# Bias addition on VectorE and x1's stores on ScalarE, instead of both on GpSimd, in a two-layer graph kernel

## Chip, cores and metric

The kernel runs on one core of a Trainium2 chip. The metric is the device time of one execution in microseconds (us), lower being better. The engines are called by the names in the profile: PE is TensorE, PEld its weight loads, DVE is VectorE, ACT is ScalarE, POOL is GpSimd and SP is SyncE, which here only issues DMAs.

## What is computed

```
h  = relu(layernorm(x))                       # x is 1250 x 1024, float32
W  = zeros(1024, 1024).at[src, dst].add(edge_weight)
x  = x + (h @ W.T + bias)                     # "x1" below
h  = relu(layernorm(x))
# two neighbour-averaging layers; A[d, s] = number of edges s -> d, deg = row sums of A
h1 = relu(h @ W_self0 + (A @ h / max(deg, 1)) @ W_neigh0 + b0)
o  = h1 @ W_self1 + (A @ h1 / max(deg, 1)) @ W_neigh1 + b1
return x + o
```

There are 40000 edges, sorted by destination. All matrices are float32.

## The kernel before

The program has four stages on one timeline. **Build** (0 to about 100 us): one-hot rows and PE matmuls turn the edge list into the columns of W and of A. The partial sums of A, 288 small windows in 45 units, are written to a DRAM scratch (`asum_scratch`). **Turn** (about 100 to 119 us): W is transposed. **Mixing** (to about 232 us): for each of 10 tiles of 128 nodes (`TN` = 10), h0 = relu(x - mean) is transposed and multiplied with W, x1 is formed, normalised into `hn`, transposed and written to `hT_scratch`. **Dense steps and layers** (to the end): each layer does its weight products in 7 x 5 steps v (`PAIRS` = 5), then the products with A.

The order on each engine is written out by hand. In the mixing it follows `mix_order()`: for tile i the steps A(i+2) (moments of x, and h0), M(i) (PE's 48 matmuls), T1(i-1) (transposes of hn), T0(i+2) (transposes of h0), B(i) (x1 and its normalisation). Each engine has its own part of each step:

- DVE in B(i), L1634 to L1645: waits for M(i) (`s_mm`) and for the biased x (`s_xb`), and from tile 2 for the store that last read this x1 buffer (`s_x1d`). It then computes x1 = bank * rstd + x in two halves (L1638), the moments of x1 (L1478 to L1483), and after ACT's square root (L899) the reciprocal (L1487) and `less` (L1645). The following A step takes the moments of a later x tile.
- ACT in B(i): issues the load of x tile i+4, takes the root, and computes hn (L927). In A it computes h0 (L921), named h in the trace. In T1(i-1) it copies the transposed hn out of PSUM (L998), stores it (L1001), and splits a weight block for the first dense steps (L1013; DVE does the other half, L1622).
- POOL adds the bias to each x tile (L792), issues the store of x1 two tiles back (`store_x1b`, L565), and makes A's additions (L783): each adds one window of the summed partials, loaded to `az` in units of 4 to 12 windows, to the table AT at an offset that it reads from a small table. `add_asums(slot)` makes the additions of one slot; slot 0 is before the mixing, slots 1 to 10 are the tiles and slots 11 to 15 the first five dense steps. `TURN_ADDS` and `MIX_ADDS` set how many additions each slot holds.
- SP issues loads in one queue. The unit loads of `az` (L670) of a slot come at that slot's place among the weight block loads (L605), and each waits until POOL has used up the unit four before it (the ring `az` has NZ = 4 buffers). The first two operand loads of the dense steps (L623, `stage<-hT_scratch`) stand in this queue behind the unit loads of slot 10.

Dense step 0 needs its operand split into two halves: ACT makes the high half (L1022), POOL the low half (L827, `operand_lo(0)`), which in POOL's order stands behind the additions of slot 10. In ACT's order `operand_hi(0)` stands in T1(8), behind hn of tile 8, and `operand_hi(1)` behind hn of tile 9. Product v is 24 matmuls (L1317). PE waits for both halves, for x1 of the tile whose PSUM banks it takes, and for the eight weight blocks.

Of the kernel before, what the change touches and what calls it, by code (L numbers as in the profile page):

```python
# [55 lines left out]
NCONST = 12 + len(set(WDS))  # L56
SETS = [(0, 8), (8, 11), (11, 13), (13, 15), (15, 17)] + [(j, j + 1) for j in range(17, NG)]
SET_OF = {j: w for w, (a, b) in enumerate(SETS) for j in range(a, b)}
TURN_ADDS = 36
MIX_ADDS = 21  # L60
FIRST_DEG = 27
EPS = 1e-5
EXACT = 4096
# [39 lines left out]
def build_program(nc, x, dst, src_cols, dst_cols, weight_cols, L0_gnn_bias, L1_gnn_W_self0, L1_gnn_W_neigh0,  # L103
# [10 lines left out]
    with ctx:  # L114
# [167 lines left out]
        s_lom = sem("s_lom")  # L282
        s_lo = sem("s_lo")
        s_mm = sem("s_mm")
        s_xb = sem("s_xb")
        s_less = sem("s_less")
        s_norm = sem("s_norm")
        s_bb = sem("s_bb")
# [271 lines left out]
            n = rows_of(i)  # L560
            eng.dma_start(x_tile(i)[0:n, :], x[NT * i:NT * i + n, :]).then_inc(s_x[i % NX], 16)

        def store_x1b(pool, i):
            pool.wait_ge(s_x1, i + 1)
            pool.dma_start(x1b_d[i], x1[:, i % 2, :]).then_inc(s_x1d[i % 2], 16)  # L565

        def store_out(pool, o):
            half, i = divmod(o - OL, TN)
# [149 lines left out]
        def _(pool):  # L718
# [66 lines left out]

            pool.wait_ge(s_tabd, 32)
            pool.wait_ge(s_built, 1)
            add_asums(0)
            pool.wait_ge(s_vec, 16)
            for i in range(TN):  # L790
                pool.wait_ge(s_h0, i + 1)
                pool.tensor_tensor(x_tile(i), x_tile(i), bias[:, :], ALU.add).then_inc(s_xb, 1)  # L792
                if i >= 2:
                    store_x1b(pool, i - 2)
                add_asums(i + 1)


            def add_operands(v):
# [64 lines left out]
            operand_lo(0)  # L863
            for layer in range(2):
                for v in range(VL * layer, VL * (layer + 1)):
                    if v < 2:
                        store_x1b(pool, TN - 2 + v)
                    if v + 1 < VL * (layer + 1) and v != VL:
                        add_operands(v + 1)
                        operand_lo(v + 1)  # L870
                    add_asums(1 + TN + v)
                    for c in blocks_at(v):
                        add_blocks(c)
                    for k in g_at(layer, v % VL - 1):
                        g_lo(k)
                for k in g_at(layer, VL - 1):
                    g_lo(k)
                for o in range(OL):
                    if layer == 1 and o == 0:
                        base_and_b1(0)  # L880
                    if layer == 1 and o >= 1:
                        store_out(pool, OL + o - 1)
                    if layer == 1 and o + 1 < OL:
                        base_and_b1(o + 1)
                    for k in g_between(layer, o):
                        g_lo(k)
                    if layer == 0 and o == OL - 1:
                        operand_lo(VL)
                        operand_lo(VL + 1)
# [5 lines left out]
        def _(act):  # L895
# [128 lines left out]
            for what, i in mix_order()[EARLY_STEPS:]:  # L1024
                if what == "A":
                    above_mean(i)
                    root_of(0, i)
                elif what == "B":
                    if i + NX < TN:
                        act.wait_ge(s_x1, i + 1)  # L1030
                        load_x(act, i + NX)
                    root_of(1, i)
                    normalize_x1(i)
                elif what == "T0":
                    h0_hi(i)
                elif what == "T1":
                    if i == TN - 2:
                        operand_hi(0)
                    hT_out(i)
                    if i < WB:  # L1040
                        block_hi(i)
# [348 lines left out]
        def _(dve):  # L1390
# [8 lines left out]
            def link(ins):  # L1399
                dve.wait_ge(s_dve, tick(ins))  # L1400
# [223 lines left out]
            for what, i in mix_order()[EARLY_STEPS:]:  # L1624
                if what == "A":
                    mix_A(i)
                elif what == "T0":
                    h0_lo(i)
                    inverse_std(0, i)
                elif what == "B":  # L1630
                    dve.wait_ge(s_mm, i + 1)
                    dve.wait_ge(s_xb, i + 1)
                    if i >= 2:
                        dve.wait_ge(s_x1d[i % 2], used(i - 2, 2))  # L1634
                        dve.wait_ge(s_hn, i - 1)
                    for half in range(2):
                        part = slice(HF * half, HF * (half + 1))
                        last = dve.scalar_tensor_tensor(out=x1[:, i % 2, part], in0=bank[2 * (i % 2) + half][0:NT, :],  # L1638
                                                        scalar=rstd[:, 0, i:i + 1], in1=x_tile(i)[:, part],
                                                        op0=ALU.mult, op1=ALU.add)  # L1640
                    last.then_inc(s_x1, 1)
                    dve.wait_ge(s_x1, i + 1)
                    moments(x1[:, i % 2, :], 1, i)
                    inverse_std(1, i)
                    dve.scalar_tensor_tensor(out=less[:, 1, i:i + 1], in0=mv[:, 1, i, 0:1], scalar=-1.0,  # L1645
                                             in1=rstd[:, 1, i:i + 1], op0=ALU.mult, op1=ALU.mult).then_inc(s_norm, 1)
                elif what == "T1":
                    if i < WB:
                        block_lo(i)
# [150 lines left out]
```

## Time and profile before

| what | value |
|---|---|
| median of 3 runs | 843.28 us (840.98 to 848.15) |
| profiled execution, its own time | 841.92 us |
| its span in the profile | 840.2 us |
| granted PE clock, mean | 0.991 of full |
| busy: PE, PEld, DVE, ACT, POOL | 799.4, 649.0, 456.5, 377.5, 431.8 us |

The span leaves out 1.7 us of the profiled execution's time. PE is busy for 95% of the span, and the other engines for 45 to 54%, so time can be saved where PE is idle or where its clock is below full.

### The profile page before, as it was taken

What the parts mean: (1) busy time and instruction counts of PE and PEld (TensorE: products, weight loads), DVE (VectorE), ACT (ScalarE), POOL (GpSimd) and SP (SyncE); (2) the same over time, 40 slices, a digit from 0 to 9 for tenths busy, and PEclk for the clock granted to TensorE, in tenths of its full rate; (3) what the DMA queues carried; (4) which work ended last, traced back from release to release, by engine and by line L of the source; (5) the groups of instructions that cost most, each with busy time, mean ns of one, the idle gap of its engine ahead of it and who ended that gap; (6) DMA issues with size and microseconds to landing.
All of it is one profiled execution on the core that took longest, in us unless ns stands there. A gap on an engine that the chain in (4) does not pass through costs nothing.

```text
span 840.2 us, 13554 instructions
## 1 busy us (share of the span) xinstructions
PE 799.4 (95%) x4660; PEld 649.0 (77%) x4661; DVE 456.5 (54%) x769; ACT 377.5 (45%) x491; POOL 431.8 (51%) x599
## 2 busy tenths in 40 slices
PE   3999999999969999999999999999999999989996
PEld 2667788888858877888877888888878887868785
DVE  7999665655532456757922453234558656224333
ACT  6755644344234322233236876453222323256652
POOL 3000047677767688765751210115888657655642
PEclk9999999999989999999999999999999999999998
DMA  3122333554376773567855543547833768666653
GB/s 107 45 68 83 92 121 115 202 174 133 123 258 190 248 251 130 168 207 252 279 185 189 191 161 114 182 136 239 293 126 113 239 220 305 217 213 189 230 179 107
DMA packets 82489, 148.58 MB, mean 177 GB/s; under 512 B 9983, under 2 KB 21366, under 8 KB 82416
## 3 DMA queue, kind: packets, MB, share of 16 engines
q1 hardware_dynamic: 62394, 102.47, 38.4%
q10 hardware_dynamic: 16982, 34.81, 11.4%
q0 software_dynamic: 3040, 10.36, 3.2%
q8 instruction: 41, 0.67, 0.3%
q14 instruction: 32, 0.26, 0.1%
HBM read 100.34 MB, written 47.27 MB: 176 GB/s over the span
## 4 chain that ended last, share of the span: by engine, by line
PE 60%; POOL 15%; issue 9%; DVE 6%; DMA 3%; ACT 3%; POOLq 1%; ACTq 1%; SPq 0%; DVEq 0%
PE bank L1317 32%; PE bank L1345 17%; POOL AT L783 6%; PE bank L1172 3%; PE bank L1161 3%; POOL T L842 2%; ACT split L1022 1%; POOL S L809 1%; PE bank L1156 1%; POOL T L844 1%; PE bank L1361 1%; DMA az<-asum_scratch 1%; DVE L L1517 1%; PE bank L1254 1%; POOLq L783 1%
## 5 line engine op out<-in xcount | busy, mean ns | idle before, releaser
L1317 PE MATMUL bank<-slot,split 128*128 128x512 f32 x1680 | 387.6, 392 | 11.3 <-ACT split L1022 10.6
L1317 PEld LDWEIGHTS bank<-slot,split 128*128 128x128 f32 x1680 | 315.5, 189 | 79.8 <-issue 14.5
L783 POOL TENSOR_TENSOR AT<-AT,az 128x50 int32 (+3 forms) x288 | 80.2, 279 | 133.3 <-DMA az<-asum_scratch 93.6
L827 POOL TENSOR_TENSOR split<-stage,split 128x512 fp32r<-128x512 f32 x50 | 64.6, 1293 | 130.7 <-ACT split L1022 130.7
L1622 DVE TENSOR_TENSOR slot<-T,slot 128x512 fp32r<-128x512 f32 x64 | 69.7, 1089 | 95.2 <-ACT slot L1013 91.8
L1052 ACT CAST Ax<-AT 128x1280 fp32r<-128x1280 uint16 x40 | 106.5, 2662 | 29.8 <-PE bank L1345 18.7
L1622 DVE TENSOR_TENSOR slot<-wst,slot 128x512 fp32r<-128x512 f32 x48 | 49.6, 1054 | 100.1 <-ACT slot L1013 100.1
L1013 ACT CAST slot<-T 128x512 fp32r<-128x512 f32 x64 | 39.8, 622 | 123.9 <-POOL T L844 92.9
L1254 PE MATMUL bank<-slot,split_m 128*128 128x512 f32 x320 | 89.4, 394 | 0.0
L1728 DVE SCALAR_TENSOR_TENSOR cst<-bank,dinv,stage 128x512 f32<-128x512 f32 x40 | 29.9, 749 | 102.8 <-PE bank L1345 69.1
L1345 PE MATMUL bank<-slot,Ax 128*128 128x512 f32 x320 | 77.1, 393 | 0.0
L1345 PEld LDWEIGHTS bank<-slot,Ax 128*128 128x128 f32 x320 | 59.3, 188 | 12.2
L1254 PEld LDWEIGHTS bank<-slot,split_m 128*128 128x128 f32 x320 | 59.0, 188 | 11.4
L844 POOL TENSOR_TENSOR T<-T,wst 128x512 f32<-128x512 f32 x48 | 61.3, 1293 | 0.0
L1022 ACT CAST split<-stage 128x512 fp32r<-128x512 f32 x50 | 31.1, 623 | 65.7 <-POOL stage L818 25.8
L1156 PE MATMUL bank<-L,R 125*128 125x100 bf16 (+3 forms) x320 | 45.7, 197 | 8.3 <-DVE L L1517 8.0
L1345 PE MATMUL bank<-g_first,Ax 128*128 128x512 f32 x200 | 49.3, 393 | 0.0
L1254 PE MATMUL bank<-WTlo,split_m 128*128 128x512 f32 x160 | 49.3, 389 | 0.0
L1161 PE MATMUL bank<-L,R 125*128 125x80 bf16 (+3 forms) x960 | 47.3, 192 | 0.1
L1156 PEld LDWEIGHTS bank<-L,R 125*128 125x128 bf16 x320 | 31.5, 98 | 20.1 <-issue 14.0
L860 POOL TENSOR_TENSOR base<-base,b 128x512 f32<-128x512 f32 x20 | 25.8, 1294 | 40.1 <-DMA base<-x1b_scratch 32.2
L1161 PEld LDWEIGHTS bank<-L,R 125*128 125x128 bf16 x960 | 43.1, 99 | 4.0 <-issue 0.2
(172 smaller groups left out, 1084.6 us busy)
## 6 DMA issues: line engine op xcount, KB each, us to landing
stage<-hT_scratch SPq DMA_DIRECT2D x90, 256.0 KB, 3.2
wst<-in_L_gnn_W_neigh SPq DMA_DIRECT2D x56, 256.0 KB, 4.3
wst<-in_L_gnn_W_self SPq DMA_DIRECT2D x56, 256.0 KB, 3.5
hT_scratch<-hTs ACTq DMA_DIRECT2D x10, 512.0 KB, 3.1
x1b_scratch<-x POOLq DMA_DIRECT2D x10, 512.0 KB, 4.1
stage<-prod0s_scratch SPq DMA_DIRECT2D x20, 256.0 KB, 2.7
hT_scratch<-h1s ACTq DMA_DIRECT2D x20, 256.0 KB, 2.1
stage<-prod1s_scratch SPq DMA_DIRECT2D x20, 256.0 KB, 2.7
```

The lines of the kernel that those rows point to most:

```text
L783: pool.tensor_tensor(a, a, az32[:, n % NZ, pairs * pos:pairs * (pos + 1)], ALU.add) \
L827: pool.tensor_tensor(split[:, v % 2, 1, :], source(v), split[:, v % 2, 0, :].bitcast(F32), ALU.subtract).then_inc(s_olo, 1)
L844: last = pool.tensor_tensor(T[:, b, :], T[:, b, :], wst[:, c % NS, :], ALU.subtract)
L1013: act.copy(slot[t % 2][:, 0, HF * b:HF * (b + 1)], block_source(c)).then_inc(s_whi, 1)
L1022: act.copy(split[:, v % 2, 0, :], source(v)).then_inc(s_ohi, 1)
L1052: act.copy(Ax[:, o % 2, :, :], ATd[:, NT * n:NT * (n + 1), :].rearrange("p d s -> p s d")).then_inc(s_ax, 1)
L1156: last = pe.matmul(a_bank(n)[:, at:at + ka(j)], row, L[:, q, c, 0:ka(j)], start=(c % SHARED[j] == 0), stop=ends)
L1161: last = pe.matmul(w_bank(j)[:, bass.ds(offsets[c // SHARED[j]], kw(j))], row, L[:, q, c, ka(j) + kw(j) * part:ka(j) + kw(j) * (part + 1)] ...
L1254: last = pe.matmul(bank[2 * (i % 2) + half][0:NT, :], split_m[:, i % 2, a, NT * k:NT * (k + 1)], WT[b][:, k, HF * half:HF * (half + 1)], s ...
L1317: last = pe.matmul(dense_bank(v, which)[:, :], split[:, v % 2, a, NT * k:NT * (k + 1)], slot[t % 2][:, b, HF * (HK * which + k):HF * (HK * ...
L1345: last = pe.matmul(ag_bank(rest_o)[:, :], Ax[:, o % 2, s, :], g_parts(half, s)[:, b, :], start=(s == 0 and b == 0), stop=(s == TN - 1 and ...
L1622: dve.tensor_tensor(lo, block_source(c), hi.bitcast(F32), ALU.subtract).then_inc(s_wlo, 1)
```

## The change

VectorE adds the bias to x in step B, ahead of its waits for the product, with a wait of its own for the result. ScalarE issues the store of x1 of the same tile, in step B, behind a wait for x1. GpSimd has neither any more: from slot 0 to 10 it makes only additions. The slots are redistributed: 40 additions in slot 0 instead of 36, 23 in each tile's slot instead of 21, and so 18 in the five dense slots together instead of 42. The same 288 additions are made. SP's unit loads move with their slots.

```diff
--- before.py
+++ after.py
@@ -56,8 +56,8 @@
 NCONST = 12 + len(set(WDS))
 SETS = [(0, 8), (8, 11), (11, 13), (13, 15), (15, 17)] + [(j, j + 1) for j in range(17, NG)]
 SET_OF = {j: w for w, (a, b) in enumerate(SETS) for j in range(a, b)}
-TURN_ADDS = 36
-MIX_ADDS = 21
+TURN_ADDS = 40
+MIX_ADDS = 23
 FIRST_DEG = 27
 EPS = 1e-5
 EXACT = 4096
@@ -282,7 +282,6 @@
         s_lom = sem("s_lom")
         s_lo = sem("s_lo")
         s_mm = sem("s_mm")
-        s_xb = sem("s_xb")
         s_less = sem("s_less")
         s_norm = sem("s_norm")
         s_bb = sem("s_bb")
@@ -560,9 +559,8 @@
             n = rows_of(i)
             eng.dma_start(x_tile(i)[0:n, :], x[NT * i:NT * i + n, :]).then_inc(s_x[i % NX], 16)
 
-        def store_x1b(pool, i):
-            pool.wait_ge(s_x1, i + 1)
-            pool.dma_start(x1b_d[i], x1[:, i % 2, :]).then_inc(s_x1d[i % 2], 16)
+        def store_x1b(eng, i):
+            eng.dma_start(x1b_d[i], x1[:, i % 2, :]).then_inc(s_x1d[i % 2], 16)
 
         def store_out(pool, o):
             half, i = divmod(o - OL, TN)
@@ -785,14 +783,8 @@
 
             pool.wait_ge(s_tabd, 32)
             pool.wait_ge(s_built, 1)
-            add_asums(0)
-            pool.wait_ge(s_vec, 16)
-            for i in range(TN):
-                pool.wait_ge(s_h0, i + 1)
-                pool.tensor_tensor(x_tile(i), x_tile(i), bias[:, :], ALU.add).then_inc(s_xb, 1)
-                if i >= 2:
-                    store_x1b(pool, i - 2)
-                add_asums(i + 1)
+            for slot_of_adds in range(TN + 1):
+                add_asums(slot_of_adds)
 
 
             def add_operands(v):
@@ -863,8 +855,6 @@
             operand_lo(0)
             for layer in range(2):
                 for v in range(VL * layer, VL * (layer + 1)):
-                    if v < 2:
-                        store_x1b(pool, TN - 2 + v)
                     if v + 1 < VL * (layer + 1) and v != VL:
                         add_operands(v + 1)
                         operand_lo(v + 1)
@@ -1026,9 +1016,10 @@
                     above_mean(i)
                     root_of(0, i)
                 elif what == "B":
+                    act.wait_ge(s_x1, i + 1)
                     if i + NX < TN:
-                        act.wait_ge(s_x1, i + 1)
                         load_x(act, i + NX)
+                    store_x1b(act, i)
                     root_of(1, i)
                     normalize_x1(i)
                 elif what == "T0":
@@ -1628,8 +1619,11 @@
                     h0_lo(i)
                     inverse_std(0, i)
                 elif what == "B":
+                    if i == 0:
+                        dve.wait_ge(s_vec, 16)
+                    dve.wait_ge(s_h0, i + 1)
+                    link(dve.tensor_tensor(x_tile(i), x_tile(i), bias[:, :], ALU.add))
                     dve.wait_ge(s_mm, i + 1)
-                    dve.wait_ge(s_xb, i + 1)
                     if i >= 2:
                         dve.wait_ge(s_x1d[i % 2], used(i - 2, 2))
                         dve.wait_ge(s_hn, i - 1)
```

ACT's order in the last two tiles, from the weight block of tile 7's step to the split of dense step 1's operand. Before:

```order
233 L1013 CAST slot0<-wst 128x512
234 L899 ACTIVATE std<-var 128x1
235 L927 ACTIVATE hn<-x1,less,rstd 128x1024
236 L1022 CAST split<-stage 128x512
237 L998 COPY hTs<-bank6 128x512
238 L998 COPY hTs<-bank7 128x512
239 L1001 DMA hT0_scratch<-hTs 128x1024
240 L899 ACTIVATE std<-var 128x1
241 L927 ACTIVATE hn<-x1,less,rstd 128x1024
242 L1022 CAST split<-stage 128x512
```

After:

```order
241 L1003 CAST slot0<-wst 128x512
242 L563 DMA x1b_scratch<-x1 128x1024
243 L889 ACTIVATE std<-var 128x1
244 L917 ACTIVATE hn<-x1,less,rstd 128x1024
245 L1012 CAST split<-stage 128x512
246 L988 COPY hTs<-bank6 128x512
247 L988 COPY hTs<-bank7 128x512
248 L991 DMA hT0_scratch<-hTs 128x1024
249 L563 DMA x1b_scratch<-x1 128x1024
250 L889 ACTIVATE std<-var 128x1
251 L917 ACTIVATE hn<-x1,less,rstd 128x1024
252 L1012 CAST split<-stage 128x512
```

A store of x1 now stands ahead of each root, behind the store of the transposed hn. On POOL, nothing but additions stands ahead of the first operand's low half any more.

DVE's order for tile 8, from `less` of tile 7. Before:

```order
366 L1645 SCALAR_TENSOR_TENSOR less<-mv,rstd 128x1
367 L1622 TENSOR_TENSOR slot0<-wst,slot0 128x512
368 L1638 SCALAR_TENSOR_TENSOR x1<-bank0,rstd,xt 128x512
369 L1638 SCALAR_TENSOR_TENSOR x1<-bank1,rstd,xt 128x512
370 L1478 BN_STATS st<-x1 128x6 x2
371 L1480 BN_AGGR mv<-st 128x2
372 L1483 TENSOR_SCALAR var<-mv 128x1
373 L1487 RECIPROCAL rstd<-std 128x1
```

After:

```order
374 L1639 SCALAR_TENSOR_TENSOR less<-mv,rstd 128x1
375 L1613 TENSOR_TENSOR slot0<-wst,slot0 128x512
376 L1625 TENSOR_TENSOR xt<-xt,bias 128x1024
377 L1632 SCALAR_TENSOR_TENSOR x1<-bank0,rstd,xt 128x512
378 L1632 SCALAR_TENSOR_TENSOR x1<-bank1,rstd,xt 128x512
379 L1469 BN_STATS st<-x1 128x6 x2
380 L1471 BN_AGGR mv<-st 128x2
381 L1474 TENSOR_SCALAR var<-mv 128x1
382 L1478 RECIPROCAL rstd<-std 128x1
```

One instruction, the bias addition over 1024 columns, has come in behind the weight block's low half and ahead of x1.

SP's order around the first operand loads (`stage<-hT0_scratch`). Before:

```order
26 L605 DMA wst<-in_L1_gnn_W_self0 128x512
27 L670 DMA az<-asum_scratch 128x480 x6
28 L670 DMA az<-asum_scratch 128x160
29 L670 DMA az<-asum_scratch 128x500 x13
30 L623 DMA stage<-hT0_scratch 128x512 x2
31 L670 DMA az<-asum_scratch 128x500
32 L605 DMA wst<-in_L1_gnn_W_neigh0 128x512 x2
33 L623 DMA stage<-hT0_scratch 128x512
```

After:

```order
26 L603 DMA wst<-in_L1_gnn_W_self0 128x512
27 L668 DMA az<-asum_scratch 128x480 x4
28 L668 DMA az<-asum_scratch 128x160
29 L668 DMA az<-asum_scratch 128x500 x18
30 L621 DMA stage<-hT0_scratch 128x512 x2
31 L603 DMA wst<-in_L1_gnn_W_neigh0 128x512 x2
32 L621 DMA stage<-hT0_scratch 128x512
33 L668 DMA az<-asum_scratch 128x500
```

Ahead of the two operand loads now stand 18 loads of the widest units where there were 13.

## Rows read from the trace of the kernel before

**Rows 1.** Windows of the whole core; columns are named in the first line.

```profile
core 0: us, PE busy (x) PEld busy (x) DVE busy (x) ACT busy (x) POOL busy (x), PEclk, DMA share, GB/s
...
110.00:232.80 122.80, 122.80 (x624) 103.58 (x622) 69.03 (x152) 48.48 (x82) 85.97 (x236) 1.00 0.46 152
232.80:240.08 7.28, 0.01 (x1) 0.03 (x1) 3.49 (x9) 4.21 (x8) 5.38 (x16) 0.84 0.74 251
240.08:253.22 13.14, 13.14 (x48) 10.60 (x49) 5.00 (x4) 3.01 (x6) 7.96 (x15) 0.83 0.78 258
253.22:327.00 73.78, 72.06 (x321) 59.18 (x319) 32.96 (x38) 25.37 (x44) 57.08 (x68) 1.00 0.66 215
```

**Rows 2.** Waits of PE in the whole span: line, releaser, us, times, longest.

```profile
PE bank L1317 <- ACT split L1022: 10.6, 4, 7.3
```

**Rows 3.** Timeline of PE: start, us, line, operation, count, idle before and releaser.

```profile
181.97 1.03 PE L1177 MATMUL bank<-ident,hn 128*128 128x128 f32 x8
...
194.61 1.03 PE L1177 MATMUL bank<-ident,hn 128*128 128x128 f32 x8
...
231.77 1.03 PE L1177 MATMUL bank<-ident,hn 128*128 128x128 f32 x8
...
240.08 13.30 PE L1317 MATMUL bank<-slot,split 128*128 128x512 f32 x48 [7.28 <-ACT split L1022]
...
254.01 43.78 PE L1317 MATMUL bank<-slot,split 128*128 128x512 f32 x192
```

**Rows 4.** Timeline of PEld, the weight loads, around 195 us.

```profile
195.38 0.90 PEld L1177 LDWEIGHTS bank<-ident,h 128*128 128x128 f32 x8
```

**Rows 5.** Timeline of POOL at the end of the mixing.

```profile
227.35 2.40 POOL L792 TENSOR_TENSOR xt<-xt,bias 128x1024 f32<-128x1024 f32 x1
229.69 0.57 POOL L565 DMA_DIRECT2D x1b_scratch<-x  x1
...
238.60 1.28 POOL L827 TENSOR_TENSOR split<-stage,split 128x512 fp32r<-128x512 f32 x1
```

**Rows 6.** Timeline of SP, the DMA issues.

```profile
173.72 58.30 SPq L670 DMA_DIRECT2D az<-asum_scratch  x20
232.11 0.86 SPq L623 DMA_DIRECT2D stage<-hT_scratch  x2
```

**Rows 7.** Timeline of ACT.

```profile
191.37 1.25 ACT L927 ACTIVATE hn<-x,less,rstd 128x1024 f32<-128x1024 f32 x1 [0.42 <-DVE less L1645]
193.00 1.15 ACT L921 ACTIVATE h<-xt,less 128x1024 f32<-128x1024 f32 x1 [0.38 <-DVE less L1482]
...
229.79 1.24 ACT L927 ACTIVATE hn<-x,less,rstd 128x1024 f32<-128x1024 f32 x1 [2.56 <-DVE less L1645]
235.04 0.62 ACT L1022 CAST split<-stage 128x512 fp32r<-128x512 f32 x1 [4.01 <-DMA stage<-hT_scratch]
```

**Rows 8.** Timeline of DVE.

```profile
185.17 0.69 DVE L1622 TENSOR_TENSOR slot<-wst,slot 128x512 fp32r<-128x512 f32 x1 [4.72 <-ACT slot L1013]
...
187.55 1.41 DVE L1638 SCALAR_TENSOR_TENSOR x<-bank,rstd,xt 128x512 f32<-128x512 f32 x2
...
227.46 2.30 DVE L1645 SCALAR_TENSOR_TENSOR less<-mv,rstd 128x1 f32<-128x1 f32 x1
232.80 1.41 DVE L1638 SCALAR_TENSOR_TENSOR x<-bank,rstd,xt 128x512 f32<-128x512 f32 x2 [3.04 <-DMA x1b_scratch<-x]
```

**Rows 9.** One line's instructions: L783 from 126 to 238.59 us.

```profile
L783 POOL TENSOR_TENSOR AT<-AT,az x210: 216/256/751, 126.0 to 238.3; 128x30 int32 x32, 128x50 int32 x31, 128x40 int32 x28, 128x20 int32 x14
```

**Rows 10.** The tile bias, and the tensor x1b_scratch, by line.

```profile
L792 POOL TENSOR_TENSOR xt<-xt,bias x8: 2377/2400/2410, 121.3 to 227.3; 128x1024 f32<-128x1024 f32 x8
...
L565 POOL DMA_DIRECT2D x1b_scratch<-x x10: 571/573/747, 145.6 to 245.2; - x10
```

**Rows 11.** Timeline of POOL, two additions that DVE's 185.17 row overlaps.

```profile
184.91 1.08 POOL L783 TENSOR_TENSOR AT<-AT,az 128x40 int32 x2
```

**Rows 12.** DVE's groups by line, 260 to 600 us, shapes apart.

```profile
L1730 DVE TENSOR_TENSOR cst<-cst,b 128x512 f32<-128x512 f32 x20 | 13.9, 693 | 0.7
```

## The prediction

> **What bounds the kernel now.** I read the windows first, then what PE waits for, then PE's timeline around its longest wait, then the other engines there.
>
> The windows [rows 1] show PE without a pause from 110 to 232.80 us. From 232.80 to 240.08 it does nothing. Then it needs 13.14 us for 48 matmuls, at a mean granted clock of 0.83, so part of that time is at the lower level of 1.2 GHz. After that it is nearly gapless at 1.00. PE's table of waits puts 10.6 us in the whole span down to L1317 and ACT's split, of which 7.3 us is this one wait [rows 2]. So the mixing is bound by PE, 12.64 us a tile (194.61 less 181.97), and the dense steps are too: 192 matmuls take 43.78 us, 5.47 us for a product of 24 [rows 3]. What can be won lies in the 20.4 us between 232.80 and 253.22: at full clock, two products need 10.94 us. That leaves 9.5 us: 7.28 idle and 2.2 of clock.
>
> Who is late there? The profile names ACT's split, but ACT had made that one by 235.66 [rows 7]. POOL makes the other half at 238.60, ending 239.88, 0.20 us before PE starts [rows 3, 5]. POOL did not wait; it came to the split when the additions ahead were done. ACT's own split was late because its operand was: SP issued that load at 232.11, at the end of 58 us in which its unit loads were paced by POOL's additions [rows 6]. ACT waited 4.01 us for it, and all that it does for tile 9 stood behind that [rows 7]. DVE too started x1 of tile 9 only at 232.80, after waiting for the store of tile 7, which POOL issued at 229.69 behind a bias addition [rows 5, 8]. All three threads lead to GpSimd being late at the end of the mixing.
>
> **GpSimd after the change.** From 126.0 to 238.6 us it made 210 additions [rows 9]. In these 112.6 us lie 9 bias additions of 2.40 us (21.6) and 8 stores of 0.57 us (4.6) [rows 10]. The rest, 86.4 us, is 0.411 us an addition with all pauses. In the changed kernel four units of 12 windows are loaded before the mixing instead of three, so 48 additions can be made before the next unit lands at about 126. 270 less 48 leaves 222, or 91.2 us, which ends at 217. DVE's new additions hold GpSimd up: while a two-input DVE instruction of 0.69 us ran, two of its additions took 1.08 us [rows 8, 11], where two at the median of 0.256 [rows 9] take 0.51; so 0.57 us, and about 1.0 us for one nearly twice as long. Nine of these make 226. SP keeps unit loads behind weight block loads until 173.7 [rows 6], which may cost another 1 or 2: 227 to 228. The low half is wanted at about 231, so 3 to 4 us are spare. The operand load, now behind 18 of the widest units instead of 13, is issued once 254 additions are made, some 16 before the end, near 221; with 3 us of transfer it is there 6 us early. Moving 24 additions forward thus costs nothing here as long as those 3 us hold. The 18 left in the dense steps lighten GpSimd where PE is the bound: nothing won.
>
> **VectorE's addition.** No row has this instruction. The nearest has two SBUF inputs and half the columns and takes 0.693 us [rows 12]; doubled it is 1.39, less a fixed part paid once. I take D = 1.25 us. The bounds are 0.69 (half the columns) and 2.40, what GpSimd needs for the same work [rows 10]. It stands in DVE's order behind the weight block and ahead of x1, so all of step B and the following step A come D later, unless DVE was waiting anyway. In a quiet tile h0 of the next but two is ready at 194.15 [rows 7] and PE loads it at 195.38 [rows 4]: 1.23 us of slack. D uses it up, and with the handover PE slips 0.1 to 0.2 us. But the chain starts at the transposes of hn (181.97) and ends one tile later: a slip gives the next chain that much more room, so it recurs every second tile. For the seven tiles concerned I count 0.3 us. For larger D the loss over the mixing is about half of (D - 1.25) in each of 8 tiles, 4 x (D - 1.25).
>
> Something is given back. In tile 8 DVE's `less`, a one-column instruction with two SBUF inputs, took 2.30 us from 227.46 and ended at 229.76, just as GpSimd's bias addition begun at 227.35 ended at 229.75 [rows 5, 8]. That blocking goes, so hn of tile 8, which ended at 231.03 [rows 7], should come about 0.8 us earlier (2.1 won, D lost), in time for its transposes at 231.77.
>
> Here a rule bears on the change. The Trainium skill, page "SBUF — State Buffer", section "Practical consequences", says that a DVE instruction with two SBUF inputs and a GpSimd instruction that reads SBUF exclude each other for a whole instruction, whichever issues first. By that rule, the 2.30 us row agrees. It speaks against the new addition as well: DVE would first sit out the addition in progress, and GpSimd then stand still for all of D. The rows at 185.17 show DVE's 0.69 us, the same as the 0.693 us mean elsewhere, in the midst of GpSimd's additions [rows 8, 11, 12], so I charge DVE nothing for this in the sum, and a rival below takes the other case.
>
> **The stores.** SP issues two loads in 0.86 us [rows 6], so I take 0.4 us for a store on ACT. From x1's end (188.96) to hn's start (191.37) [rows 7, 8] ACT has only a load to issue and one root to take, so this costs nothing in a tile, and x1's buffer comes free two tiles early. In tile 9 the store follows the transposed hn's, still ahead of the root.
>
> **The end of the mixing, new.** PE ends the hn transposes at 232.80 as before (all times plus the 0.3 slip). ACT's high half of operand 0, behind hn of tile 8, is ready by 230.9, GpSimd's low half by 232.2. The rest that product 0 needs, x1 of tile 8 and eight weight blocks, comes ahead of hn of tile 8 in DVE's order. So it starts at 232.8, no longer at 240.08, and ends at 238.27. What is late next is product 1's operand, behind hn of tile 9. DVE can begin x1 at 232.0, right after the matmuls. From x1's start to hn's end a quiet tile takes 5.07 us (187.55 to 192.62) [rows 7, 8]: 237.1. ACT's split of 0.62 gives 237.7, GpSimd's 1.28 [rows 5] gives 239.0, the handover of 0.2 gives 239.2. PE pauses 0.9 us. Product 1 ends at 239.2 + 5.47 = 244.67, where before it was 253.22. I count on the clock staying up: it did after the pauses of 1.7 us in all between 253 and 327 [rows 1]. Of the 9.5 us, 8.55 are won; with the slip of 0.3 the gain is 8.25. Steps behind this wait on PE's progress, on rings and on each other in the same way as before, so all shifts as one.
>
> The profiled execution took 841.92 us, so 833.7 by its own time. The median shown is 1.36 us above it: 843.28 - 8.25 = **835.0 us**.
>
> **Rivals.**
> *GpSimd still late.* At 0.45 us an addition, or with more blocking, it reaches the low half near 235. Each microsecond beyond 231 costs one: gain 4.5, 838.8 us. For it: the 0.411 has pauses I can't place. Against: only at 238.6 would all be lost.
> *The port rule in full.* DVE sits out up to one addition of 0.26 us (the median in [rows 9]) before each bias addition: D = 1.5, 1 us more of slips: 836.0. The page is the one named above.
> *VectorE becomes the mixing's bound, and the kernel slower.* The place is h0 for PE's transposes. By the formula the gain is gone at D = 3.3 us. At D = 3.9, if a bias addition took as long as GpSimd's and half as much again in waits, the loss is 10.6 and the time 845.6. At D = 2.4 it is 4.6: 839.6. Against it: 0.693 us for half of it.
> *The wait does not go.* Another thread (weight blocks, transfers on ACT's queue, now with 512 KB more a tile) holds product 0 back by several us: 841 to 844. The DMA share, 0.74 in the idle window [rows 1], speaks a little for it, though five unit loads leave that neighbourhood.
> *More than counted.* No slips, product 1 in time: 833.8. If earlier stores and lighter dense steps also close the later pauses of 1.7 us: 832.1.
>
> **Chances.** The forecast, 834 to 836: 0.51. GpSimd late: 0.12. The port rule: 0.10. VectorE partly (to 843): 0.05; wholly (slower than before): 0.05. The wait stays: 0.07. More than counted: 0.10. A measurement of this kernel tells about 1% (8.4 us) from no change, and the forecast lies on that edge, at 0.98%. I give half of it to each side: faster by over 1% 0.26 + 0.10 + 0.02 = 0.38; slower by over 1% 0.04, from VectorE's case; the same 0.58. The range reaches down to 832 and up to 841, which leaves out the wait that stays and VectorE as the bound.
>
> **What would show it.** In the profile after: PE's wait near 233 us under 1 us and one of about 1 us near 238; no window at 0.83 clock behind it; GpSimd reaching its first split before 231; the first operand loads issued near 221; DVE's new line at 1.2 to 1.3 us; per-tile period of PE 12.65 to 12.75. A DVE mean above 2 us, a period above 13, or operand loads after 229 would make the prediction wrong.

## The result, and the profile after

| kernel | median | range of 5 runs | ratio to before, 95% interval |
|---|---|---|---|
| before | 843.28 us | 840.98 to 848.15 | |
| changed | 835.17 us | 832.46 to 837.49 | 0.9898 [0.9856, 0.994] |

The change makes the kernel 1.0% faster; 835.0 us was forecast. The profiled execution took 833.53 us with a span of 831.8, against 841.92 and 840.2: 8.4 us less in both.

Windows of the changed kernel:

```profile
core 0: us, PE busy (x) PEld busy (x) DVE busy (x) ACT busy (x) POOL busy (x), PEclk, DMA share, GB/s
...
131.00:233.00 102.00, 102.00 (x515) 86.01 (x514) 63.66 (x133) 40.58 (x69) 62.81 (x208) 1.00 0.54 170
233.00:246.00 13.00, 12.36 (x60) 9.84 (x58) 6.40 (x12) 6.63 (x12) 6.00 (x10) 1.00 0.70 244
246.00:831.80 585.80, 569.74 (x2537) 466.65 (x2534) 282.59 (x354) 250.39 (x287) 319.03 (x262) 0.99 0.60 198
```

Where the kernel before had a window of 7.28 us without work and one at a clock of 0.83 [rows 1], PE is now busy for 12.36 of the 13.00 us between 233 and 246, at 1.00. From 246 on nothing has changed: from the transposes of hn of tile 9 to the end of the span it is 831.8 - 245.20 = 586.6 us here and 840.2 - 253.22 = 587.0 before. So the whole gain lies between the hn transposes of tiles 8 and 9, 21.45 us before (253.22 less 231.77 [rows 3]) and 12.95 now. PE's timeline shows it:

```profile
131.65 1.03 PE L1168 MATMUL bank<-ident,hn 128*128 128x128 f32 x8
...
220.47 1.03 PE L1168 MATMUL bank<-ident,hn 128*128 128x128 f32 x8
...
232.25 1.03 PE L1168 MATMUL bank<-ident,hn 128*128 128x128 f32 x8
233.28 5.73 PE L1308 MATMUL bank<-slot,split 128*128 128x512 f32 x24
239.65 5.71 PE L1308 MATMUL bank<-slot,split 128*128 128x512 f32 x24 [0.64 <-POOL split L819]
245.20 1.03 PE L1168 MATMUL bank<-ident,hn 128*128 128x128 f32 x8
```

Product 0 follows the transposes without a wait, and the one pause is 0.64 us ahead of product 1. From tile 0's transposes (131.65) to tile 8's (232.25) it takes 100.60 us; before it was 100.39 (131.38 to 231.77).

The other engines. POOL's timeline at the end of the mixing:

```profile
221.07 6.16 POOL L781 TENSOR_TENSOR AT<-AT,az 128x50 int32 x14 [0.91 <-POOL AT L781]
231.79 1.28 POOL L819 TENSOR_TENSOR split<-stage,split 128x512 fp32r<-128x512 f32 x1 [4.56 <-ACT split L1012]
238.23 1.28 POOL L819 TENSOR_TENSOR split<-stage,split 128x512 fp32r<-128x512 f32 x1 [5.16 <-ACT split L1012]
```

Its additions end at 227.2, and now it waits 4.56 us for its first split, where before it went there straight from the additions at 238.60 [rows 5]. SP's timeline:

```profile
174.14 45.66 SPq L668 DMA_DIRECT2D az<-asum_scratch  x23
219.90 1.14 SPq L621 DMA_DIRECT2D stage<-hT_scratch  x2
```

The loads of the first two operands leave at 219.90 instead of 232.11 [rows 6]. DVE's and ACT's timelines, in this order:

```profile
229.76 1.22 DVE L1625 TENSOR_TENSOR xt<-xt,bias 128x1024 f32<-128x1024 f32 x1
232.50 1.41 DVE L1632 SCALAR_TENSOR_TENSOR x<-bank,rstd,xt 128x512 f32<-128x512 f32 x2 [1.52 <-PE bank L1245]
...
229.88 1.24 ACT L917 ACTIVATE hn<-x,less,rstd 128x1024 f32<-128x1024 f32 x1 [0.42 <-DVE less L1639]
231.03 0.61 ACT L1012 CAST split<-stage 128x512 fp32r<-128x512 f32 x1
...
236.32 1.24 ACT L917 ACTIVATE hn<-x,less,rstd 128x1024 f32<-128x1024 f32 x1 [0.43 <-DVE less L1639]
```

The bias addition of tile 9 (229.76) lies in DVE's idle time. Its x1 starts at 232.50, held by PE and no longer by the store of tile 7 [rows 8], and hn of tile 9 ends at 237.56. ACT's first split no longer waits for a transfer. The bias addition by line, and POOL's waits for its unit loads from 115 us on (us in total, times, longest):

```profile
L1625 DVE TENSOR_TENSOR xt<-xt,bias x8: 1218/1225/1305, 123.6 to 229.8; 128x1024 f32<-128x1024 f32 x8
...
POOL AT L781 <- DMA az<-asum_scratch: 11.6, 4, 4.3
```

### The profile page after: what moved, and what is told of

It reads as the page before. It is cut to its first block, busy times and chain, and to the rows that moved or that the text cites. A ratio compares the mean times of both kernels' runs of the same rounds, so it can differ in the third digit from the quotient of the medians.

```text
span 831.8 us, 13561 instructions
## 1 busy us (share of the span) xinstructions
PE 797.8 (96%) x4660; PEld 647.4 (78%) x4661; DVE 460.8 (55%) x779; ACT 377.2 (45%) x491; POOL 409.1 (49%) x579
## 4 chain that ended last, share of the span: by engine, by line
PE 74%; POOL 9%; DVE 7%; issue 4%; ACT 2%; DMA 2%; ACTq 1%; POOLq 0%; SPq 0%; DVEq 0%
PE bank L1308 34%; PE bank L1336 15%; PE bank L1245 13%; PE bank L1163 3%; PE bank L1152 3%; POOL T L834 2%; PE bank L1168 2%; POOL base L852 2%; POOL slot L844 1%; POOL S L801 1%; PE bank L1147 1%; ACT split L1012 1%; DVE L L1508 1%; PE bank L1352 1%; DVE degs L1652 1%
## 5 line engine op out<-in xcount | busy, mean ns | idle before, releaser
L781 POOL TENSOR_TENSOR AT<-AT,az 128x50 int32 (+3 forms) x288 | 83.4, 290 | 140.2 <-DMA az<-asum_scratch 102.9
L1147 PEld LDWEIGHTS bank<-L,R 125*128 125x128 bf16 x320 | 31.5, 98 | 20.1 <-issue 13.8
L1336 PE MATMUL bank<-g_mid,Ax 128*128 128x512 f32 x160 | 41.9, 405 | 4.9 <-ACT Ax L1043 3.7
```

The lines of the kernel that those rows point to most:

```text
L781: pool.tensor_tensor(a, a, az32[:, n % NZ, pairs * pos:pairs * (pos + 1)], ALU.add) \
L1147: last = pe.matmul(a_bank(n)[:, at:at + ka(j)], row, L[:, q, c, 0:ka(j)], start=(c % SHARED[j] == 0), stop=ends)
L1336: last = pe.matmul(ag_bank(rest_o)[:, :], Ax[:, o % 2, s, :], g_parts(half, s)[:, b, :], start=(s == 0 and b == 0), stop=(s == TN - 1 and ...
```

## The experiments

Each was measured in turns with the kernel before on the same chip. The kernel before had medians of 844.94 us beside e1 to e4, 844.05 beside e5, e6, e8 and e10, and 843.34 beside e7, e9 and e11, so runs of different groups are compared by their ratios. The spread between executions of one kernel is 0.4 to 1.2%, so where 1 or 2 us matter I go by the traces, above all by the time from tile 8's hn transposes to tile 9's on PE, called **the gap** below: 21.45 us before, 12.95 with the change. Behind tile 9's transposes the thirteen traces differ as well: from there to the end of the span it is 585.5 us (e2) to 591.0 (e4). So a trace tells a microsecond up to that place, and not over the whole span. The expected texts call the length of VectorE's bias addition D.

| run | what | median | ratio to before, 95% interval | gap |
|---|---|---|---|---|
| e1 | bias on VectorE only | 836.96 | 0.9914 [0.9889, 0.9939] | 12.99 |
| e2 | stores on ScalarE only | 836.16 | 0.9911 [0.9878, 0.9944] | 13.05 |
| e3 | both, old numbers | 836.46 | 0.9903 [0.987, 0.9936] | 12.98 |
| e4 | new numbers only | 846.51 | 1.0017 [0.9994, 1.0039] | 24.57 |
| e5 | change, one more DVE instruction | 842.07 | 0.998 [0.9959, 1.0002] | 13.84 |
| e6 | change, two more | 855.42 | 1.0142 [1.009, 1.0194] | 16.03 |
| e7 | change, bias addition earlier | 834.23 | 0.9887 [0.985, 0.9923] | 12.97 |
| e8 | e7 and e9 together | 832.92 | 0.9887 [0.9843, 0.9931] | 11.78 |
| e9 | change, second high half earlier | 831.65 | 0.9857 [0.9825, 0.989] | 11.95 |
| e10 | change, all additions in the mixing | 834.3 | 0.9882 [0.985, 0.9915] | 12.99 |
| e11 | before, operand loads earlier | 846.42 | 1.004 [1.0008, 1.0072] | 23.60 |

### e1 to e4: the parts

e1 takes the change with TURN_ADDS 36 and MIX_ADDS 21, and gives the stores back to GpSimd (cut here: the last two stores, which go into the dense steps as before, and ScalarE's, which are taken out):

```diff
             for i in range(TN):
+                if i >= 2:
+                    pool.wait_ge(s_x1, i - 1)
+                    store_x1b(pool, i - 2)
                 add_asums(i + 1)
...
```

> VectorE adds the bias, but GpSimd still issues x1's stores, and the slots keep 36 and 21 additions. Theory A (GpSimd's lateness at the end of the mixing is what was removed, and the bias additions are most of it): nine bias additions of 2.40 us gone, some 9 us of blocking added back, and 24 additions fewer to make, so GpSimd is still through before 231 us and product 0 starts near 233.3 as in the changed kernel. Time 834 to 837. Rival B (the stores on ScalarE carry the gain, since they free x1's buffer early): the wait of 3 us for the buffer of tile 7 stays, product 0 or 1 is late by some us, 839 to 843.

e2 is its counterpart, with the old numbers too: ScalarE stores, GpSimd adds the bias. Against the kernel before (cut where three points stand):

```diff
                 pool.tensor_tensor(x_tile(i), x_tile(i), bias[:, :], ALU.add).then_inc(s_xb, 1)
-                if i >= 2:
-                    store_x1b(pool, i - 2)
                 add_asums(i + 1)
...
                 elif what == "B":
+                    act.wait_ge(s_x1, i + 1)
                     if i + NX < TN:
-                        act.wait_ge(s_x1, i + 1)
                         load_x(act, i + NX)
+                    store_x1b(act, i)
```

> ScalarE issues the stores of x1, but GpSimd still adds the bias, and the slots keep 36 and 21 additions. Theory A: GpSimd saves eight stores of 0.57 us, 4.6 us, and perhaps some pauses around them; it reaches its first split near 234 instead of 238.6, product 0 starts near 235.5 with less time at the lower clock, 837.5 to 840. Rival B (the early release of x1's buffer carries the gain): 834 to 836.

e3 only puts the numbers back.

```diff
-TURN_ADDS = 40
-MIX_ADDS = 23
+TURN_ADDS = 36
+MIX_ADDS = 21
```

> Both moves of the change, but with 36 and 21 additions as before, so that 42 instead of 18 are left to the dense steps. Theory A (PE is the bound of the dense steps, GpSimd has room there): no difference from the changed kernel, 834 to 836.5, with GpSimd through about 10 us earlier at the end of the mixing. Rival C (the redistribution earns part of the gain by lightening the dense steps): 837 to 840.

e4 is the kernel before with the new numbers.

```diff
-TURN_ADDS = 36
-MIX_ADDS = 21
+TURN_ADDS = 40
+MIX_ADDS = 23
```

> The kernel before with 40 and 23 additions and nothing moved. Theory A (each microsecond that GpSimd is late at the end of the mixing is a microsecond of PE's wait): 24 more additions of 0.411 us in front of the first split, 9.9 us, so product 0 starts near 250 and the time is 852 to 855. Rival D (something else holds product 0, such as the stores or the weight blocks): within 3 us of the kernel before, 841 to 846.

e1 came out as expected: product 0 starts at 232.65 and the time is 836.96 us. So did e3 in time, 836.46: redistributing the additions earns nothing. (GpSimd's additions end there at 222.83, 4.4 us before those of the changed kernel and not 10, in part since it waits 12.6 us for units instead of 11.6 and has 6.7 us of long pauses instead of 3.8.) e2 did not: moving the stores alone gives the whole gain. Its trace, POOL and then PE:

```profile
232.35 1.27 POOL L824 TENSOR_TENSOR split<-stage,split 128x512 fp32r<-128x512 f32 x1
...
231.75 1.03 PE L1173 MATMUL bank<-ident,hn 128*128 128x128 f32 x8
233.83 11.13 PE L1313 MATMUL bank<-slot,split 128*128 128x512 f32 x48 [1.05 <-DVE x L1634]
244.80 1.03 PE L1173 MATMUL bank<-ident,hn 128*128 128x128 f32 x8
```

GpSimd comes to its first split at 232.35, 6.25 us earlier than before. Eight stores are 4.6 us. Of the rest, 1.4 us are shorter pauses ahead of every sixteenth addition: 13.8 us from 126 us to the split instead of 15.2. The long ones among them ("issue" in the table of waits) are 2.5 us instead of 6.7, the short ones 11.3 instead of 8.5. Why fewer are long is not shown; e3 has no stores either and has 6.7 us of long ones. The split is late enough for product 0 to start at 233.83, half a microsecond later than with the change, but product 1 follows without a pause, and tile 9's transposes start 13.05 us after tile 8's. GpSimd need not be on time by 231, then. Whatever lets it begin that split by about 233 brings the same, since product 1's operand is what comes last. Rival B names the early release of x1's buffer, and its range, 834 to 836, is nearer to the time of e2. But e1 keeps the stores on GpSimd and has a gap of 12.99, so moving them isn't needed; GpSimd's time is what e1 and e2 have in common. The trace puts product 0's wait down to an x1 of VectorE. It can't be: product 0 needs x1 only up to tile 8, and the one that VectorE made just before (231.95 to 233.36) is tile 9's. In the changed kernel product 0 starts at 233.28, before tile 9's x1 ends at 233.91.

e4 missed by far, and its time of 846.51 us lies nearer to rival D's range. Its POOL, then PE (cut at 256.3 us):

```profile
241.33 1.27 POOL L827 TENSOR_TENSOR split<-stage,split 128x512 fp32r<-128x512 f32 x1
...
242.81 13.47 PE L1317 MATMUL bank<-slot,split 128*128 128x512 f32 x46 [9.77 <-ACT split L1022]
```

Against the kernel before, GpSimd's split is 2.73 us later (241.33 for 238.60 [rows 5]) and product 0 is 2.73 us later (242.81 for 240.08 [rows 3]): one to one, as expected. It is the 2.7 that I had at 9.9. Twelve of the 24 additions are made before 126 us in time in which GpSimd waited before, for the bias and for the first unit of the mixing; the prediction had counted that for the changed kernel, and I forgot it here. The other half would cost 4.9 at 0.411 each, of which 2.2 were made up: the long pauses are 4.0 us up to the split where the kernel before has 6.7. By itself e4 doesn't decide against the operand load, since ScalarE's split starts 3.25 us later too (238.29). That takes e11.

### e10 and e11: is it GpSimd's own work?

e11 changes the kernel before in SP's order alone:

```diff
             for i in range(TN):
+                if i == TN - 1:
+                    load_operand(0)
+                    load_operand(1)
                 for n in units_begun_in(i + 1):
                     load_asum(n)
-            load_operand(0)
-            load_operand(1)
```

> The kernel before with one thing moved: SP issues the first two operand loads ahead of the unit loads of slot 10. Theory A (GpSimd's own work is what product 0 waits for): the load lands ten us earlier and ScalarE no longer waits for it, but the low half still comes behind the additions, at or after 239.9, so product 0 starts at 240 and the time is that of the kernel before, 842 to 845. Rival K (the late operand load, which ScalarE waited 4.0 us for, is the cause): product 0 starts near 235 to 236, 838 to 840.

ACT, POOL and PE of e11, in this order:

```profile
231.28 0.60 ACT L1023 CAST split<-stage 128x512 fp32r<-128x512 f32 x1
...
238.41 2.96 POOL L784 TENSOR_TENSOR AT<-AT,az 128x50 int32 x6 [2.48 <-issue]
241.33 1.25 POOL L828 TENSOR_TENSOR split<-stage,split 128x512 fp32r<-128x512 f32 x1
...
232.12 1.03 PE L1178 MATMUL bank<-ident,hn 128*128 128x128 f32 x8
242.80 13.08 PE L1318 MATMUL bank<-slot,split 128*128 128x512 f32 x48 [9.65 <-issue]
```

ScalarE makes its split at 231.28, four microseconds earlier than before, and waits for no transfer. PE starts no earlier for it, but 1.5 us after GpSimd's split begins, as in the kernel before (238.60 and 240.08) and in e4 (241.33 and 242.81). Rival K is out. The time, 846.42 us, lies above both ranges. That fits GpSimd as well: ahead of its last six additions it paused for 2.48 us, where before it was 0.91, these six took 2.96 us instead of 2.11, and it came to the split 2.73 us later.

One relation holds in all the traces in which product 0 waits. It starts 0.20 to 0.22 us after the end of GpSimd's split: at 240.08 in the kernel before, 242.81 in e4 and 242.80 in e11, 233.83 in e2 and 234.53 in e10, and 241.43 and 253.44 in e5 and e6 below. ScalarE's split doesn't move with it: it ends 4.4 us ahead of product 0 in the kernel before and 10.9 in e11.

The late operand load and the late x1 of tile 9 were real waits behind the same cause; ending one of them was worth nothing.

e10 gives GpSimd all 288 additions before its first split.

```diff
-TURN_ADDS = 40
-MIX_ADDS = 23
+TURN_ADDS = 48
+MIX_ADDS = 24
```

> The changed kernel with 48 and 24 additions, so that all 288 are made before the first operand split. Theory A (GpSimd was through 4.6 us before its operand in the changed kernel, and what it is later than that PE waits one to one): 18 more additions at 0.4 us are 7.3 us; product 0 starts 2 to 3.5 us later than 233.3, time 836.5 to 839. Rival G (the additions have room, since GpSimd's pauses shrink when it has more to do): no change, 834 to 836.5.

Its POOL and PE:

```profile
225.20 7.89 POOL L781 TENSOR_TENSOR AT<-AT,az 128x50 int32 x17
233.04 1.27 POOL L819 TENSOR_TENSOR split<-stage,split 128x512 fp32r<-128x512 f32 x1
...
232.56 1.03 PE L1168 MATMUL bank<-ident,hn 128*128 128x128 f32 x8
234.53 11.18 PE L1308 MATMUL bank<-slot,split 128*128 128x512 f32 x48 [0.93 <-DVE x L1632]
245.55 1.03 PE L1168 MATMUL bank<-ident,hn 128*128 128x128 f32 x8
```

The additions end at 233.09, 5.9 us later than in the changed kernel, and the split comes straight after. Product 0 waits 0.93 us for it, and then product 1 doesn't wait at all: the gap is 12.99 us. The pause ahead of product 1 has moved ahead of product 0. So GpSimd has the 4.6 us that it waits in the changed kernel and one more, and Theory A was wrong: product 0 starts 1.25 us later, not 2 to 3.5, and tile 9's transposes no later at all. The time, 834.3 us, lies in rival G's range and agrees with the changed kernel's. The 18 additions cost 5.9 us and not 7.3; what shrinks is the wait for units (7.1 us instead of 11.6), not the pauses.

### e5 and e6: what VectorE's instruction may cost

Behind each bias addition stands one more (e6: two more) instruction that leaves x as it is:

```diff
                     link(dve.tensor_tensor(x_tile(i), x_tile(i), bias[:, :], ALU.add))
+                    link(dve.tensor_tensor(x_tile(i), x_tile(i), x_tile(i), ALU.max))
```

> The changed kernel with one more VectorE instruction behind each bias addition: the larger of x and x, over the same 1024 columns with two SBUF inputs, which leaves the result as it is and brings D from 1.22 to about 2.47 us. Theory A (the slack of a tile is 1.23 us, a slip gives the next chain room, so half of what is beyond it is paid per tile): 4 x 1.25 = 5 us slower than the changed kernel, a period of about 13.2 us a tile, time 839 to 841. Rival E (paid in full in every tile): 8 x 1.25 = 10 us, 844 to 846. Rival F (VectorE has more room than the slack I read): within 1.5 us of the changed kernel, 834 to 837.

> The same with two more instructions, D about 3.7 us. Theory A: 4 x 2.5 = 10 us slower than the changed kernel, a period of about 13.9 us, time 844 to 847, so as slow as before the change. Rival E: 20 us, 854 to 857. Rival F: under 840.

The time of e5, 842.07 us, lies between Theory A's range and rival E's, and that of e6, 855.42, in rival E's. Rival F is out in both. Not all of e6's loss is VectorE's, as the clock below shows. ACT, then DVE, then PE in e5:

```profile
186.46 1.15 ACT L911 ACTIVATE h<-x_fourth,less 128x1024 f32<-128x1024 f32 x1 [0.39 <-DVE less L1473]
...
187.61 1.05 ACT L988 COPY hTs<-bank 128x512 f32<-128x512 f32 x2
...
201.35 1.05 ACT L988 COPY hTs<-bank 128x512 f32<-128x512 f32 x2
...
190.69 1.29 DVE L1488 TENSOR_TENSOR split_m<-bank,split_m 128x512 fp32r<-128x512 f32 x2 [0.25 <-ACT split_m L925]
192.09 1.32 DVE L1625 TENSOR_TENSOR xt<-xt,bias 128x1024 f32<-128x1024 f32 x1
193.45 1.22 DVE L1626 TENSOR_TENSOR xt<-xt 128x1024 f32<-128x1024 f32 x1
194.71 1.41 DVE L1633 SCALAR_TENSOR_TENSOR x<-bank,rstd,xt 128x512 f32<-128x512 f32 x2
...
186.13 1.09 PE L1168 MATMUL bank<-ident,hn 128*128 128x128 f32 x8
...
199.87 1.09 PE L1168 MATMUL bank<-ident,hn 128*128 128x128 f32 x8 [0.20 <-ACT hn L917]
201.41 1.09 PE L1168 MATMUL bank<-ident,h 128*128 128x128 f32 x8 [0.44 <-ACT h L911]
```

PE in e6:

```profile
133.66 1.09 PE L1168 MATMUL bank<-ident,hn 128*128 128x128 f32 x8 [0.72 <-ACT hn L917]
...
193.15 1.09 PE L1168 MATMUL bank<-ident,hn 128*128 128x128 f32 x8 [1.35 <-ACT hn L917]
194.69 1.75 PE L1168 MATMUL bank<-ident,h 128*128 128x128 f32 x8 [0.44 <-ACT h L911]
...
237.89 1.09 PE L1168 MATMUL bank<-ident,hn 128*128 128x128 f32 x8 [1.32 <-ACT hn L917]
```

The tiles come every 13.57 us in e5 (132.10 to 227.07 over seven) and every 14.89 in e6 (133.66 to 237.89), against 12.69 in the changed kernel (131.65 to 220.47). The reason stands in ACT's and DVE's rows of e5. The copy of the transposed hn (187.61) starts right behind h0 (186.46 + 1.15), not behind PE's transposes, which ended at 187.22, and x1 (194.71) right behind the added instruction. So there is a loop without PE in it: ScalarE's copy, block and split, VectorE's low half, bias, x1, moments, ScalarE's hn and h0, and again the copy. In the kernel before this copy, on ACT's timeline, stands at

```profile
183.04 1.08 ACT L998 COPY hTs<-bank 128x512 f32<-128x512 f32 x2 [1.38 <-PE bank L1177]
```

and from there to the end of h0 (194.15 [rows 7]) it is 11.11 us. D, with its handovers (from the bias addition's start to x1's, 1.26 us for each instruction), comes on top: 11.11 + 2.52 = 13.63 and 11.11 + 3.78 = 14.89. The period of a tile is the greater of PE's 12.65 and 11.1 + D. It fits all four kernels: with D = 1.26 the loop takes 12.4.

The gap grows too, to 13.84 us in e5. The later hn of tile 8 holds up ScalarE's first split, which stands behind it, and so GpSimd's, which comes at 239.64 after 4.57 us of waiting. In e6 (16.03 us) PE's clock adds to it. PE waits 0.7 to 1.4 us ahead of the hn transposes of seven of the nine tiles there; from 193 to 200 us the granted clock was 0.76, and product 0 took 7.09 us instead of 5.73. In e5 it stayed at 1.00 from 133 to 253 us.

### e7, e9 and e8: the two pauses that are left

e7 puts the bias addition where VectorE waits for ScalarE, between the moments of tile i+2 and the block (cut: the same four lines leave step B):

```diff
...
+                elif what == "M":
+                    if i == 0:
+                        dve.wait_ge(s_vec, 16)
+                    dve.wait_ge(s_h0, i + 1)
+                    link(dve.tensor_tensor(x_tile(i), x_tile(i), bias[:, :], ALU.add))
                 elif what == "T1":
```

> The changed kernel with VectorE's bias addition alone moved to the start of the tile's step. Theory A: the transposes of hn come at 12.65 us from tile to tile without slips, so tile 8's start 0.2 to 0.5 us earlier than in the changed kernel; the pause ahead of product 1 stays, or is up to 0.3 us longer. Time 834 to 836, not to be told from the changed kernel's; a gain above 1 us would speak for the addition having been on the path in more places than seen.

e9 makes the high half of the second operand behind the first one's (cut: it is left out at its old place, behind hn of tile 9):

```diff
                     if i == TN - 2:
                         operand_hi(0)
+                        operand_hi(1)
...
```

> The changed kernel with the second operand's high half alone moved ahead. Theory A: product 1 starts straight behind product 0; from tile 8's hn transposes to tile 9's it is 11.8 to 12.0 us instead of 12.95. Time 833.5 to 835.5. Rival H: the pause moves to a later step and nothing is won.

e8 has both edits.

> The changed kernel with VectorE's bias addition moved ahead, to the start of the tile's step where VectorE waits for ScalarE, and with the second operand's high half made directly behind the first one's, ahead of the last transposed hn. Theory A: the addition is off the path to h0, so PE's slips of 0.5 us over the mixing go, and the pause of 0.64 us ahead of product 1 goes; the transposes of tile 9's hn start near 243.7 instead of 245.2, time 833 to 835, which the time alone will hardly tell from the changed kernel. Rival H (the moved split delays the transposed hn and the weight blocks behind it): a new pause of 0.5 us or more in dense steps 1 to 4, no gain.

In e7 the transposes of hn come every 12.65 us and tile 8's start 100.30 us after tile 0's instead of 100.60: 0.3 us won, the slips. (Counted from the start of the span they begin at 232.41, 0.16 later than in the changed kernel, because tile 0's came 0.46 later, at 132.11.) The pause ahead of product 1 is 0.92 us. In e9:

```profile
232.09 1.03 PE L1169 MATMUL bank<-ident,hn 128*128 128x128 f32 x8
233.04 11.17 PE L1309 MATMUL bank<-slot,split 128*128 128x512 f32 x48
244.04 1.03 PE L1169 MATMUL bank<-ident,hn 128*128 128x128 f32 x8
```

PE does 48 matmuls in one stretch; the gap is 11.95 us instead of 12.95. In e8 it is 11.78, and the mixing is without slips too (131.57 to 231.87, 100.30 us). Up to tile 9's transposes the traces give e8 1.5 us over the changed kernel (243.65 for 245.20) and e9 1.2. No new pause shows up in the dense steps behind: in e8 and e9, as in the changed kernel, PE's first one comes 73 us later (1.37, 1.43 and 1.37 us). Rival H is out. In time e9 has the best ratio, 0.9857, and e8 0.9887, with intervals that overlap each other and the changed kernel's. Nor do whole spans tell them apart: the span is 830.9 us in e8's trace and 833.4 in e9's, against 831.8. In e9's the rest behind tile 9's transposes is 2.8 us longer than the changed kernel's, and one thing that differs is the granted clock: below 1.00 in two stretches of 100 us (0.98 from 444, 0.99 from 644), where the changed kernel's has one (0.98 from 645). So e8 and e9 are faster than the kernel before beyond doubt, and ahead of the changed one only as far as tile 9's transposes; a gain in the whole time over the changed kernel is not shown.

## Why the prediction was right

**The bound and the cause held.** GpSimd's lateness at the end of the mixing held PE back, and the 9.5 us of idle time and clock were what could be won. e4 and e11 show it one to one, and e2, e5, e6 and e10 start product 0 at the same 0.2 us behind GpSimd's split. The shown path is GpSimd's low half; the late operand load, which the trace suggests as the cause, was none (e11).

**The terms of the sum**, predicted and measured: D 1.25 and 1.22 us; product 0 at 232.8 plus 0.3, and 233.28; the pause ahead of product 1 0.9, and 0.64; tile 9's transposes at 244.67 plus 0.3, and 245.20; slips 0.3, and 0.21 over the mixing, with 0.27 more from before its start; the gain 8.25, and 8.4 in span. The clock stayed at 1.00 behind the short pause.

**GpSimd's timetable came out right by luck, from two wrong terms.** Forecast was the end of the additions at 227 to 228, measured 227.2. But I charged 9 us for VectorE's instructions holding it up, and the 288 additions together took 83.4 us instead of 80.2, 3.2 us more. And I charged 1 or 2 us for waits on units behind SP's weight blocks, where the table of waits shows 11.6, of which 4.3 is the first, which the sum had as its start: 7.3 us. The forecast of the time didn't hang on it: in e10 the additions end at 233.09 and the gap is the same.

**The port rule.** The ten bias additions took 1.218 to 1.305 us, median 1.225. The wait of up to 0.26 us that the Trainium skill's rule ("SBUF — State Buffer", "Who interferes with whom", the list "Practical consequences") would add ahead of it shows as 0.08 us at most, in the longest of them. For a long GpSimd instruction VectorE did wait, as the row of 2.30 us shows [rows 8]. The rule's other side, GpSimd standing still, shows in full. DVE and POOL around 150 us:

```profile
149.87 1.23 DVE L1625 TENSOR_TENSOR xt<-xt,bias 128x1024 f32<-128x1024 f32 x1
149.95 1.24 POOL L781 TENSOR_TENSOR AT<-AT,az 128x30 int32 x1
```

This one addition of GpSimd took 1.24 us instead of some 0.25 and ended 0.10 us after VectorE's. Five of the ten bias additions met GpSimd like this, with one addition of 1.14 to 1.24 us each, so about 0.9 us lost each time. That is the size which the prediction gave it (1.0). What was wrong was the count of nine: the others fell for the most part into times in which GpSimd waited or paused, or had no additions to make.

**What was wrong beside the forecast.** First, "each microsecond beyond 231 costs one": the first 2 us cost nothing, since product 1's operand comes last anyway (e2, e10). Second, "the loss over the mixing is about 4 x (D - 1.25)" and "the gain is gone at D = 3.3": the loop on ScalarE and VectorE is paid in full once 11.1 + D exceeds 12.65, so the gain is gone near D = 2.6 over eight tiles, and e5 with 2.5 is at 0.998 of before. I had let the chain start at PE's transposes and not seen that it closes without PE. The forecast didn't rest on it, but the slower rival was nearer than I held it to be. Third, the change's parts: the prediction took them together, while either move alone is enough (e1, e2) and the new numbers earn nothing (e3).

The last is also where part of the expected gain "went": GpSimd was freed of 24 us of bias additions and 6 us of stores, and some 6 of them are all that PE can use.

## What to carry to other kernels

When one late engine holds several threads, find the one that really starts the waiting engine by shifting each alone; the trace's releaser was here the wrong one. Count how much of a relief can be used before the next operand is the last: a move that brought GpSimd to its split 6 us earlier (e2) did as much as one that took 24 us of bias additions from it (e1). And before an instruction goes onto an engine with slack, sum up the loops that close without the bound engine, not only the slack at its waits: this one had room for 1.5 us, and each microsecond beyond that cost a microsecond in every tile.

## What the runs showed of the hardware that was not expected

GpSimd pauses in its sequence of short additions, mostly ahead of every sixteenth one, where the kernel reads the next 16 offsets from a table. Most of these pauses are 0.9 to 1.0 us. The ones that the table of waits calls "issue", 1.05 to 2.73 us, lie at the same places in all thirteen traces: the number of additions ahead of each is a multiple of 16. Up to the first split they add up to 2.5 us (e2) to 9.1 us (e11), with and without the stores. One of them, 2.48 us in e11 where before it was 0.91, was part of what moved the end of the mixing. So the place is known; why the same reading sometimes takes up to three times as long stays open.

When a two-input VectorE instruction of 1.22 us started shortly before one of GpSimd's short additions, that addition took up to 1.24 us, while VectorE lost 0.08 us at most. The price was GpSimd's alone.

Pauses of PE of about the same length went with different clocks. In e5 one of 1.31 us ahead of product 0 left the granted clock at 1.00 (239 to 253 us); in e6, with pauses of 1.3 us ahead of the hn transposes in most tiles, it fell to 0.76 between 193 and 200 us.
